# A decoder layer with a mixture of experts: half of the down layer's expert blocks come by SyncE transfers from memory

## What is computed

```python
def kmoe(x_flat, W_router, A, B, scale, bias, ..., top_k):
    logits = x_flat @ W_router.T
    vals, idx = jax.lax.top_k(logits, top_k)          # 2 of 64 experts for each token
    probs = jax.nn.softmax(vals, axis=-1)
    Ag, Bg = A[idx], B[idx]
    Y = jnp.einsum('nkoi,nij,nkpj->nkop', Ag, xs, Bg)
    out = jnp.einsum('nkop,nk->nop', Y, probs)
    return out * scale + bias
y = kmoe(gelu(kmoe(x, ..up..)), ..down..)
```

## Time and profile before

| | |
|---|---|
| median of 3 runs | 2172.82 us (2169.03 to 2178.83) |
| the profiled execution, its own time | 2180.39 us |
| its span, first to last instruction | 2178.5 us |
| busy: PE, DVE, ACT, POOL | 89%, 59%, 57%, 13% |
| granted TensorE clock, mean | 0.927 |
| transfers after the start | about 10 GB/s |

### The profile page before, as it was taken

The page is one execution under the profiler, slowest core; times in us unless marked ns, Lnnn a source line. Parts: engine busy times, 40 slices in busy tenths (PEclk is TensorE's granted clock), DMA queues, the critical chain, the costliest instruction groups (busy, mean ns, idle before and its releaser), DMA issues.

```text
span 2178.5 us, 47368 instructions
## 1 busy us (share of the span) xinstructions
PE 1947.4 (89%) x13298; PEld 1458.5 (67%) x13298; DVE 1283.8 (59%) x5457; ACT 1252.4 (57%) x4007; POOL 277.6 (13%) x593
## 2 busy tenths in 40 slices
PE   7998988989898989988989889888989999899975
PEld 5767667675766757667676676767767577675754
DVE  1456555666565666656565556665656656566664
ACT  2475564757556485564755547565474755648553
POOL 3020200203021030200202002020110302102010
PEclk9998999999999898989989899898998989989887
DMA  7000000000000000000000000000000000000000
GB/s 226 1 11 1 7 11 8 11 2 16 2 7 11 7 11 1 7 11 8 11 2 7 11 8 11 2 16 2 7 11 2 16 2 7 11 7 2 1 6 6
DMA packets 18600, 27.65 MB, mean 13 GB/s; under 512 B 2178, under 2 KB 17027, under 8 KB 17923
## 3 DMA queue, kind: packets, MB, share of 16 engines
q1 hardware_dynamic: 18274, 23.84, 3.4%
HBM read 19.65 MB, written 4.19 MB: 11 GB/s over the span
## 4 chain that ended last, share of the span: by engine, by line
PE 63%; DVE 14%; issue 12%; ACT 4%; DVEq 3%; POOL 2%; ACTq 1%; POOLq 0%
PE G L788 7%; PE O L732 5%; PE G L759 5%; PE PT L690 4%; PE G L815 4%; PE S L719 3%; PE S L717 3%; PE S L632 3%; DVE chosen_dn L275 2%; PE S L642 2%; DVE yT L1042 2%; DVE shared L908 2%; PE FA L801 2%; PE PT L672 2%; ACT chosen_up L262 1%
## 5 line engine op out<-in xcount | busy, mean ns | idle before, releaser
L508 ACT ACTIVATE shared<-shared,neg_max 128x128 f32<-128x128 f32 (+1 forms) x512 | 204.9, 447 | 297.8 <-DVE neg_max L908 296.4
L262 ACT COPY chosen_up<-experts 32x128 f32 x1024 | 251.6, 291 | 44.9 <-issue 38.5
L788 PE MATMUL G<-chosen_up,W 128*64 128x256 f32 x1024 | 260.5, 394 | 8.0 <-DVE pre L1032 8.0
L908 DVE CUSTOM_DVE_ANT_0 shared<-S,neg_bias 128x128 f32<-128x128 f32 (+1 forms) x512 | 162.4, 355 | 127.7 <-PE S L719 122.1
L690 PE MATMUL PT<-ident,shared 128*128 128x128 f32 x768 | 161.0, 326 | 77.9 <-DVE shared L901 65.1
L275 ACT COPY chosen_dn<-experts 64x64 f32 x1024 | 197.7, 240 | 52.9 <-issue 36.5
L275 DVE COPY chosen_dn<-experts 64x64 f32 x1024 | 152.4, 189 | 67.6 <-issue 57.5
L262 DVE COPY chosen_up<-experts 32x128 f32 x768 | 171.9, 255 | 32.3 <-issue 27.1
L388 POOL TENSOR_SCALAR var_eps<-moments 128x2 f32<-128x2 f32 x48 | 10.4, 217 | 1355.7 <-DVE moments L845 1345.5
L1032 DVE SCALAR_TENSOR_TENSOR pre<-G,scale_up,bias_up 64x256 f32<-64x256 f32 x256 | 123.2, 481 | 87.5 <-PE G L788 79.8
L815 PE MATMUL G<-chosen_dn,W 128*32 128x64 f32 x2048 | 157.5, 237 | 18.5 <-DVE W L1019 18.5
(11 more groups left out here) (164 smaller groups left out, 3819.4 us busy)
## 6 DMA issues: line engine op xcount, KB each, us to landing
x<-in_x SPq DMA_DIRECT2D x16, 256.0 KB, 2.7
ctxT<-in_ctxT SPq DMA_DIRECT2D x16, 256.0 KB, 2.9
out<-xn SPq DMA_DIRECT2D x16, 256.0 KB, 3.1
neg_bias<-in_neg_bias SPq DMA_DIRECT2D x1, 2048.0 KB, 13.3
wk<-in_xWk SPq DMA_DIRECT2D x1, 1024.0 KB
wo<-in_xWo SPq DMA_DIRECT2D x1, 1024.0 KB
wv<-in_xWv SPq DMA_DIRECT2D x1, 1024.0 KB, 7.7
wq<-in_xWq SPq DMA_DIRECT2D x1, 1024.0 KB, 9.7
```

Source lines behind the costliest of these rows:

```text
L262: last = copy(dst, src.rearrange("p (m c) -> p m c", m=2))
L508: act.activation(probs[i % 3][:, lo:hi], probs[i % 3][:, lo:hi], ACT.Exp, bias=neg_max[:, i % 3, rt:rt + 1], scale=-1.0).then_inc(probs_re ...
L788: mm = pe.matmul(G[g % 2 * F1:(g % 2 + 1) * F1, 0:n], up_W(g)[:, k * F1:(k + 1) * F1], chosen_up[g % UP_SLOTS][:, k * n:(k + 1) * n], star ...
L908: dve.tensor_tensor_reduce(probs[i % 3][:, lo:hi], S[i % 2][:, lo:hi], neg_bias[:, i, (1 - rt) * P:2 * P], 1.0, TOP, ALU.add, ALU.min, neg ...
```

## The change

The units of each group of the down layer are renumbered so that 0 to 7 are the even tokens' and 8 to 15 the odd tokens'. DVE copies units 0 to 3, ACT 4 to 7. SyncE brings 8 to 15, not from the table on chip but from the same table in memory, with one transfer for each unit, whose source address is a register value: 64 rows of two pieces of 32 numbers (128 bytes). Each of the three buffers has a semaphore of its own, which PE awaits before L801 of the group. DVE writes a third part of `offsets`, SyncE loads its 32 values by TENSOR_LOAD and waits for `second_done` before it reuses a buffer. The number of blocks that must be there, and what PE multiplies, stays.

```diff
-            "dve": {"up": range(1, 4), "dn": range(0, 8)},
-            "act": {"up": range(4, 8), "dn": range(8, 16)}}
+            "dve": {"up": range(1, 4), "dn": range(0, 4)},
+            "act": {"up": range(4, 8), "dn": range(4, 8)},
+            "sp": {"up": range(0, 0), "dn": range(8, 16)}}
+DN_TOKEN = (0, 2, 4, 6, 1, 3, 5, 7)
...
             for unit in units:
-                n, k = divmod(unit, TOPK)
+                place_of, k = divmod(unit, TOPK)
+                n = DN_TOKEN[place_of]
...
+        def fetch_dn(sp, held, g, units):
+            to = chosen_dn[g % DN_SLOTS]
+            for unit in units:
...
+                dst = to[half * F1:(half + 1) * F1, a:a + D1]
+                dst = bass.AP(dst.tensor, dst.offset, [dst.ap[0], [b - a, 2], [1, D1]])
+                src = t["experts_dn"][:, bass.ds(held[g % LOADED, unit], 2 * D1)]
+                sp.dma_start(dst, src.rearrange("p (m c) -> p m c", m=2)).then_inc(fetched_dn[g % DN_SLOTS], 16)
...
+            def choose(c, n_part):
+                n, part = n_part
+                g = n - UP_GROUPS
+                if g < 0 or part > 0:
+                    return
+                fetch_offsets(held, mybir.EngineType.SP, n, "sp")
+                if g >= DN_SLOTS:
+                    hold(sp, passed, second_done, at(c, GROUPS, n - DN_SLOTS + 1))
+                elif g == 0:
+                    sp.wait_ge(zeroed, 1 + UP_SLOTS + DN_SLOTS)
+                fetch_dn(sp, held, g, CHOOSERS["sp"]["dn"])
...
             load(1)
+            go({"route_dn": route_dn, "choose": choose}, 0, None)
             with sp.Fori(0, BATCH - 2) as c:
                 load(c + 2)
+                go({"route_dn": route_dn, "choose": choose}, c + 1, c)
                 store(c)
...
                 pe.wait_ge(chosen_act, at(c, GROUPS, UP_GROUPS + g + 1))
+                pe.wait_ge(*fetched_by(c, g))
```

More of the change, by code:

```diff
@@ L205, in decoder_layer @@
         chosen_act, chosen_dve, chosen_pool = sem("chosen_act"), sem("chosen_dve"), sem("chosen_pool")
+        fetched_dn = [sem(f"fetched_dn{i}") for i in range(DN_SLOTS)]
         zeroed, x2_biased = sem("zeroed"), sem("x2_biased")
@@ L241, in fetch_offsets @@
             layer, g, step = ("up", n, 2 * F1) if n < UP_GROUPS else ("dn", n - UP_GROUPS, 2 * D1)
-            if g % LOADED:
+            units, first = share_of(name, layer)
+            if g % LOADED or len(units) == 0:
                 return
-            units, first = share_of(name, layer)
             first += g * len(units)
@@ L276, in choose_dn, with fetched_by @@
             return last
+        def fetch_dn(sp, held, g, units):
+            to = chosen_dn[g % DN_SLOTS]
+            for unit in units:
+                place_of, k = divmod(unit, TOPK)
+                n = DN_TOKEN[place_of]
+                u, half = n // 2, n % 2
+                a, b = ((u * TOPK + k) * 2 + half) * D1, A_DN + (u * TOPK + k) * D1
+                dst = to[half * F1:(half + 1) * F1, a:a + D1]
+                dst = bass.AP(dst.tensor, dst.offset, [dst.ap[0], [b - a, 2], [1, D1]])
+                src = t["experts_dn"][:, bass.ds(held[g % LOADED, unit], 2 * D1)]
+                sp.dma_start(dst, src.rearrange("p (m c) -> p m c", m=2)).then_inc(fetched_dn[g % DN_SLOTS], 16)
+        def fetched_by(c, g):
+            uses = [len(range(slot, DN_GROUPS, DN_SLOTS)) for slot in range(DN_SLOTS)][g % DN_SLOTS]
+            each = 16 * len(CHOOSERS["sp"]["dn"])
+            return fetched_dn[g % DN_SLOTS], at(c, uses * each, (g // DN_SLOTS + 1) * each)
         def both_halves(run, eng):
@@ L366, in _, with route_dn @@
             sp.dma_start(scale_dn[:, :], t["scale_dn"].to_broadcast([P, 1])).then_inc(ffn_tables, 16)
+            held = {}
+            def choose(c, n_part):
[9 more added lines that the diff above has]
+                fetch_dn(sp, held, g, CHOOSERS["sp"]["dn"])
+            def route_dn(c):
+                hold(sp, passed, offsets_ready, at(c, 2, 2))
             load(1)
+            go({"route_dn": route_dn, "choose": choose}, 0, None)
             with sp.Fori(0, BATCH - 2) as c:
                 load(c + 2)
+                go({"route_dn": route_dn, "choose": choose}, c + 1, c)
                 store(c)
+            go({"route_dn": route_dn, "choose": choose}, BATCH - 1, BATCH - 2)
             store(BATCH - 2)
+            go({"route_dn": route_dn, "choose": choose}, None, BATCH - 1)
             store(BATCH - 1)
@@ L972, in route_keep @@
                 of = G[0:1, 256:384].rearrange("p (g u) -> p g u", g=groups)
+                by_half = G[0:1, 256:384].rearrange("p (g t half k) -> p half g t k", g=groups, half=2, k=TOPK)
                 for name in CHOOSERS:
@@ L976, in route_keep @@
                         to = offsets[:, start:start + groups * len(units)].rearrange("p (g u) -> p g u", g=groups)
-                        last = dve.tensor_copy(to, of[:, :, units.start:units.stop])
+                        if layer == 0:
+                            last = dve.tensor_copy(to, of[:, :, units.start:units.stop])
+                        else:
+                            half, first = divmod(units.start // TOPK, DN_TOK // 2)
+                            some = by_half[:, half, :, first:first + len(units) // TOPK, :]
+                            last = dve.tensor_copy(to.rearrange("p g (t k) -> p g t k", k=TOPK), some)
                 last.then_inc(offsets_ready, 1)
```

## The result

| | before | changed |
|---|---|---|
| median | 2175.75 us (2169.03 to 2178.83) | 2309.01 us (2302.86 to 2312.15) |
| ratio to before | | 1.060, 95% interval 1.057 to 1.063 |
| span of the profiled execution | 2178.5 us | 2304.3 us |
| granted TensorE clock, mean | 0.927 | 0.898 |

The medians are of four runs each. The kernel became 6% slower, 133 us. The forecast was 2066 us, 5% faster; the range ended at 2180. The result lies within 13 us of the rival "SP is the new bound" (2296).

What follows compares the result with a forecast made beforehand. PE and DVE were taken as together near the bound. Stalls 2.6, clock 4.2 and pace 1.0 give 7.8 us a batch, 117 in 15; 2180.4 - 117 + 11 (drain) = 2074, less 7.6 to the median: 2066 us, range 2022 to 2180.

Steps and rivals of the forecast that it cites:

- SP is the new bound: Rival, chance 0.16: at 0.77 us an issue the last group lands 10 us late at L801; 2296 us.
- The new transfers: SP's 64 issues a batch at 0.52 us each, 4.2 us a group; no PE wait in the overlapped batches.
- the wait's beginning: Issue time above which PE would wait for transfers at L801 in the overlapped batches: 0.61 us.
- bk to bv: Distance between two earlier transfers of small pieces on SP, taken as upper bound of an issue: 0.77 us.
- When PE asks: PE reaches L801 of group 0 at 309.1, then every 5.2 us; group 7 at 345.5.
- Shorter register loads: DVE loads 16 values instead of 32; L901 and PE come 1.30 us earlier at two places, 2.6 us a batch.
- The clock and the pace: Head stage: fewer clock falls after PE's gaps, 4.2 us a batch; 0.15 us less a head pair, 1.0 a batch.
- the three terms: Gain a batch: shorter register loads 2.6, clock 4.2, pace of a pair 1.0; together 7.8 us.
- SP's load and the landing: SP's register load of 32 values taken at 2.0 us, twice a batch; a 16 KB transfer lands in 2.2 us.
- The transfer engines: At 53 ns a piece a new transfer takes at most 0.48 us, below 0.52, so they keep up with SP.
- The page of the Trainium skill: Counter-evidence: small transfers dominated by descriptors; 64 at 0.7 us in sequence would come 5 us late a batch.
- The drain: Last batch, where nothing covers SP: 4.1 + 4.9 + 2.0 = +11.0 us; +27 at 0.77 us an issue.

Runs made afterwards that it cites:

- e4: Changed kernel with 80 more SyncE transfers behind its end, eight series of ten in different shapes; 64 rows started 0.633 us apart at register and fixed addresses alike.
- e1: Changed kernel without the odd tokens' transfers and without PE's wait for them (those tokens multiplied by zeros): 2035.3 us, 0.933 of the kernel before.
- e9: Changed kernel with each SyncE transfer bringing 48 of the 64 rows, same number of transfers and waits: 2047.9 us, 0.939 of the kernel before.
- e2: Changed kernel with transfers landing in an unread buffer; SyncE awaits each group's landing, PE does not wait: 2128.6 us, 0.977 of the kernel before.
- e14: Changed kernel with eight series of ten fixed-address transfers behind its end, seven row counts from 40 to 80; 63 rows took 317 ns an issue, 72 rows 369.
- e6: Changed kernel with GpSimd instead of SyncE bringing the odd tokens' eight blocks, by copies from the on-chip table: 2127.6 us, 0.976 of the kernel before.

## Why the prediction was wrong

**The step that failed** is "I take 0.52 with the register instruction", under "The new transfers". It measured 0.76: 0.60 for the issue and 0.16 for the register instructions. The prediction's own figures put the wait's beginning at 0.61 and the break-even near 0.70, so all hung on this one number, and it was read from the wrong rows. The transfers of `x` and `ctxT` were chosen because they stand in the loop at a register address; but they have 128 rows, and the new ones 64. The trace of before held a nearer row, the load of the whole down table into 64 rows, beside the other table's into 32 (timeline of SP, start and issue time):

```profile
14.58 0.43 SPq L364 DMA_DIRECT2D experts<-in_experts_up  x1
15.05 0.55 SPq L364 DMA_DIRECT2D experts<-in_experts_dn  x1
```

0.55 for an issue of 64 rows, with the 0.10 that lie between the end of x's issue and the start of ctxT's, is 0.65, above 0.61 already. The upper bound of 0.77, bk to bv, was right to a hundredth, but its two issues took 0.72 and 0.70, so its agreement is by chance. The reason given against that rival, "all issues at a register address", counted the wrong property: e4 shows the address to cost nothing in the issue.

**When PE asks** was taken wrong as well, with less weight. The prediction has PE ask every 5.2 us up to group 7, 45.5 us after the offsets. But groups 6 and 7 come faster: in e1's batch at full clock they start 4.32 and 2.81 us after the group ahead of them, group 7 42.0 us after the offsets, and the trace of before had 2.80 between the two as well (350.61 and 353.41). With the measured loads and landing the wait so begins near (42.0 - 3.7 - 2.0) / 64 = 0.57 us for an issue, not 0.61.

**What followed is the rival's mechanism.** In the batch shown DVE has written the offsets at 309.28 (timeline of DVE):

```profile
308.87 0.41 DVE L1029 CAST offsets<-G 1x32 int32<-1x32 f32 x3 [0.98 <-PE G L810]
```

Group 7 starts at 366.56, 57.3 us later, for two loads of 1.87, 64 x 0.763 = 48.8, some issues of up to 1.1 us, and 2.0 to land. The rival had 55.5 by the same sum. In e1 group 7 starts 42.0 us after the offsets in the batch at full clock and 48.0 in the one in which the clock falls, so the changed kernel's is 15.3 or 9.3 late. Of the 261 us between the changed kernel and e9, the drain has 16.6: group 0 waits 10.46 us against 7.97, and groups 0 to 7 take 46.2 us against 32.1. The other 244 are 16.3 us a batch; the rival had 10 + 4.2 = 14.2, lateness and clock.

**Shorter register loads**: right. DVE's load of 16 values took 1.10 us (1.11 forecast), the stalls became 0.98 and 0.47 (about 1.2 and 0.6 forecast).

**The clock and the pace**: right in kind, set too low. e1 has 9.6 us a batch for the sum of the three terms, near the upper bound of 10.3, and 0.27 us less a pair where 0.15 was taken. Some falls remain after the first stall, as allowed for: a mean of 0.968. PE's wait for DVE at this place fell from 65.1 us to 21.8 in e1, 2.9 a batch (2.6 in the sum); 6.5 pairs at 0.27 are 1.8. As an estimate this leaves 4.9 a batch for the clock, where 4.2 was taken; no run changes clock and pace separately.

**SP's load and the landing**: 1.87 and 2.0 us, against 2.0 and 2.2. **The transfer engines**: right that they keep up; e2 shows no cost to PE from the traffic in the head stage. The 53 ns for a piece were far too much: in the changed kernel 9063 packets between 311 and 365 us took 12.4% of 16 engines, 12 ns each.

**The page of the Trainium skill** (DMA: Bandwidth & Descriptors, section Bandwidth) was weighed as something that spoke against the change, with 5 us of lateness a batch at 0.7 us a transfer. The direction was right, but by another cause: the lateness was in SP's issue, and the transfers' own 2.0 us to landing overlapped. The prediction left out that the page's table is of transfers issued from GpSimd to 128 partitions, so it bore on this case less than it seemed.

**The drain**: forecast +11, or +27 at 0.77. PE idles 10.46 us before group 0 instead of 4.30, and groups 0 to 7 take 46.2 us instead of 24.5: +27.9, as the sum gives it with the measured issue.

## What to carry to other kernels

A transfer that is hidden can still cost: count the issuing engine's time for the exact shape, with its register instructions, times the number, against the time at which the consumer wants the last one, and read it from the row that has the same number of rows. Take work from the engine for which others wait, give SyncE only as many transfers as fit (here 4 of 16 units, with 8 on ACT, 2046 us, where 8 and 4 gave 2309), and look at what else is queued behind them, such as the store. Where a forecast hangs on one price near its threshold, give the other side more than 0.16.

## What the runs showed of the hardware

- The time to issue a transfer doesn't follow its size or its rows: 0.597 us for 64 rows, 0.317 for 63, 0.43 for 128 (e4, e14). But for 64, it follows the largest number up to 16 that divides the rows: 0.295 us for 8 to 0.42 or 0.43 for 16. Leaving out 16 rows of 64 made the kernel 11% faster.
- An issue of 64 rows took 0.545 us at a register address in a series by itself, with its pieces joined, and 0.599 in the loop, with two pieces. One of 48 rows took 0.42 in a series and 0.316 in the loop.
- A DVE copy of 0.19 us was held for up to 2.3 us while GpSimd worked through a row of copies from the same table (e6).
- Behind a stall of PE of 0.98 to 0.99 us the granted clock was 0.50, so 1.2 GHz, in some batches (e1, 297.5 to 308 us) and 1.00, so 2.4 GHz, in others (e1, 421 to 469 us); what decides is open.
